# A two-layer graph kernel: row gathers, weight loads, fills and scatter lag of the first layer re-timed

## The reference, cut to what matters

```python
h = relu(layernorm(x))
x = x + layer0(h)      # x_norm = layernorm(h) * g + b
                       # q, k, v = x_norm @ Wq.T + bq, ...; dk, dv = silu(edge_attr @ Wd.T + bd)
                       # attn = silu(sum(q[dst] * k[src] * dk)) * cosine_cutoff(edge_weight)
                       # h + segment_sum(v[src] * dv * attn, dst) @ Wo.T + bo
h = relu(layernorm(x))
x = x + layer1(h)      # relu((A_norm @ (h @ W) + b) @ W1 + b1) @ W2 + b2, self-loops, symmetric norm
```

## Time and profile before

| what | us |
|---|---|
| median of 3 timed runs | 1825.09 (1824.55 to 1827.22) |
| the profiled execution's own time | 1813.87 |
| its span on the core | 1812.2 |
| PE busy | 1607.8 (89%) |
| DVE busy | 1424.0 (79%) |
| POOL busy | 1214.8 (67%) |
| ACT busy | 1127.9 (62%) |

### The profile page before, as it was taken

One profiled execution on the slowest core, in us unless ns is written; L12 is line 12 of the kernel. 1 busy time (PEld: TensorE's weight loads), 2 busy tenths in 40 slices (PEclk: granted clock), 3 DMA queues, 4 the chain that ended last, 5 costly groups with the idle time before them and its releaser, 6 DMA issues.

```text
span 1812.2 us, 29106 instructions
## 1 busy us (share of the span) xinstructions
PE 1607.8 (89%) x6406; PEld 1097.8 (61%) x6406; DVE 1424.0 (79%) x5625; ACT 1127.9 (62%) x2142; POOL 1214.8 (67%) x864
## 2 busy tenths in 40 slices
PE   6999999999999927677675099999999999999998
PEld 3556666666666615455553066677666666666776
DVE  8887877777777539888785788888888888888873
ACT  2345566666666402222222398889998889888884
POOL 5325888888887457888887766666666666666650
PEclk9999999999999968888887599999999999999999
DMA  9999666666666736656655889999999999999971
GB/s 373 417 416 342 158 188 195 191 183 184 184 192 194 206 73 117 116 127 112 128 110 107 201 222 268 265 272 271 266 272 265 273 264 271 267 264 270 274 223 77
DMA packets 148029, 398.73 MB, mean 220 GB/s; under 512 B 20144, under 2 KB 56756, under 8 KB 147974
## 3 DMA queue, kind: packets, MB, share of 16 engines
q1 hardware_dynamic: 88038, 278.61, 44.5%
q0 software_dynamic: 56416, 115.46, 33.8%
q10 hardware_dynamic: 3520, 4.07, 0.7%
HBM read 217.84 MB, written 180.23 MB: 220 GB/s over the span
## 4 chain that ended last, share of the span: by engine, by line
PE 53%; POOL 20%; DMA 11%; DVE 9%; issue 6%; SPq 1%; ACT 0%; POOLq 0%; DVEq 0%; ACTq 0%
PE bank L1394 11%; PE bank L1383 11%; POOL sums_dram L504 9%; PE bank L1278 8%; DMA out_dram<-cg 6%; PE bank L1271 4%; PE bank L1285 4%; PE bank L1320 4%; POOL kept L601 4%; POOL cg L508 4%; POOL b_rs L500 3%; PE bank L1373 3%; DMA sums_dram<-ub,sidx 2%; PE bank L1259 2%; DVE cg L995 2%
## 5 line engine op out<-in xcount | busy, mean ns | idle before, releaser
L1394 PE MATMUL bank<-w_sb,kept 128*128 128x256 f32 x1568 | 354.3, 379 | 0.0
L1383 PE MATMUL bank<-kept,w 128*128 128x512 f32 x784 | 353.3, 593 | 0.0
L601 POOL TENSOR_TENSOR kept<-kept 128x1024 f32<-128x1024 f32 x98 | 232.3, 2370 | 177.1 <-DVE cg L995 177.1
L1394 PEld LDWEIGHTS bank<-w_sb,kept 128*128 128x128 f32 x1568 | 298.1, 190 | 81.7 <-issue 46.3
L1347 PE MATMUL bank<-cg,en 128*128 128x256 f32 x386 | 130.4, 482 | 121.7 <-ACT cg L1148 67.1
L500 POOL TENSOR_TENSOR b_rs<-b_ve,minus_half 128x8 f32<-128x8 f32 x102 | 210.3, 2062 | 28.2 <-DVE b_ve L1012 28.2
L1383 PEld LDWEIGHTS bank<-kept,w 128*128 128x128 f32 x784 | 141.8, 191 | 140.9 <-issue 140.9
L1186 ACT ACTIVATE kept<-kept,b_nb,b_rs 128x256 f32<-128x256 f32 x392 | 202.2, 588 | 22.0 <-DVE b_nb L985 22.0
L1176 ACT ACTIVATE kept<-kept,b_nb,b_rs 128x256 f32<-128x256 f32 x392 | 202.3, 589 | 10.2 <-DVE b_nb L985 10.2
L504 POOL DMA_INDIRECT sums_dram<-ub,sidx x96 | 156.2, 1627 | 53.8 <-issue 27.0
L1347 PEld LDWEIGHTS bank<-cg,en 128*128 128x128 f32 x386 | 93.0, 248 | 153.8 <-issue 136.7
(11 more groups left out here) (179 smaller groups left out, 3355.8 us busy)
## 6 DMA issues: line engine op xcount, KB each, us to landing
sums_dram<-cg SPq DMA_DIRECT2D x196, 512.0 KB, 15.2
kept<-in_x_dram SPq DMA_DIRECT2D x97, 512.0 KB, 6.0
kept<-sums_dram POOLq DMA_DIRECT2D x97, 512.0 KB, 10.0
cg<-sums_dram SPq DMA_DIRECT2D x97, 512.0 KB, 8.5
out_dram<-cg SPq DMA_DIRECT2D x97, 512.0 KB, 10.0
row_k<-keys_dram SPq DMA_DIRECT2D x24, 256.0 KB, 4.5
row_s<-in_src_dram SPq DMA_DIRECT2D x24, 256.0 KB, 4.3
row_d<-in_dst_dram SPq DMA_DIRECT2D x41, 128.0 KB, 3.9
```

Source lines behind the costliest of these rows:

```text
L601: pool.tensor_tensor(X1[k.slot(8)], X[k.slot(4)], H[k.slot(2)], ALU.add).then_inc(g_xh, 1)
L1383: ins = pe.matmul(bank[:, 2 + m, :], w01[:, c, m * P:(m + 1) * P], hT[k.slot(2)][:, c * GN:(c + 1) * GN], start=(c == 0), stop=(c == KC - 1))
L1394: ins = pe.matmul(to, rT[k.slot(2)][:, c * GN + j * P:c * GN + (j + 1) * P], w2_sb[:, c, :], start=False, stop=(c == KC - 1), skip_group_c ...
```

## The change

Five things are edited. Between them they move no product, and leave the second and third stage alone.

- **Gathers ahead.** The destination rows (`kept`) of pairs 10 to 18 are gathered in POOL's steps 4 to 8, two pairs a step (one in step 8), behind the power; steps 10 to 18 gather the source rows alone. Source and destination rows get semaphores of their own, and DVE waits for the second only before it reads them.
- **Late weights.** `w2` (256 KB) and `b2_rows` (512 KB) are loaded by ACT's queue in step 14, not at the start.
- **Fills.** The `sums1` fills start with SP's step 10, three a step for 32 steps, and two more behind that.
- **Scatters.** The lag is 9 pairs up to POOL's step 24, which scatters two pairs, then 8; step 40 scatters two pairs again, then the lag is 7. The loop over p ends two steps earlier.
- **DVE's loop** is split in two, since what it waits for changes at pair 19.

```diff
 SCATTER_LAG = 9
+CATCH_UP = (24, 40)
+AHEAD_FROM, AHEAD_TO, AHEAD_STEP = 10, 19, 2
...
+            def fill_sums1(at, count):
+                for i in range(count):
+                    sp.dma_start(sums1[bass.ds(at + i * GN, GN), :].rearrange("(p j) d -> p (j d)", j=G),
+                                 rows_0).then_inc(s_fill1, 16)
...
-            run_steps(sp, EP, LATER, 2, LOADED - LATER, load_edges, start=LATER)
+            full = NG // 3 // 2 * 2
+            with sp.Fori(LOADED // 2, (LOADED + full) // 2) as reg:
+                for u in range(2):
+                    s = Step(u, reg, 2)
+                    load_pair(sp, s)
+                    fill_sums1(s.value(-LOADED, 3 * GN), 3)
+            fill_sums1(full * 3 * GN, NG - full * 3)
+            for k in range(LOADED + full, EP):
+                load_pair(sp, Step(k))
...
                     gather(XS[k % 4], x, node_i[:, k, 1:2], last_node, m_x[p % 2])
-                    gather(kept[:, k, :], x, node_i[:, k, 0:1], last_node, m_x[p % 2])
+                    if not AHEAD_FROM <= p < AHEAD_TO:
+                        gather(kept[:, k, :], x, node_i[:, k, 0:1], last_node, m_k[p % 2])
+
+            def gather_ahead(p):
+                first = AHEAD_FROM + AHEAD_STEP * (p - 4)
+                for k in range(2 * first, 2 * min(first + AHEAD_STEP, AHEAD_TO)):
+                    gather(kept[:, k, :], x, node_i[:, k, 0:1], last_node, m_ahead)
+
+            def scattered(p):
+                return min(EP, max(0, p - SCATTER_LAG + sum(p > c for c in CATCH_UP)))
...
-                k = p - SCATTER_LAG
-                if 0 <= k < EP:
+                if 4 <= p < AHEAD_FROM:
+                    gather_ahead(p)
+                for k in range(scattered(p), scattered(p + 1)):
...
-            for p in range(EP + SCATTER_LAG):
+            for p in range(EP + SCATTER_LAG - len(CATCH_UP)):
...
-                    dve.wait_ge(m_x[q], a.turns(2, 64))
+                    dve.wait_ge(m_x[q], a.turns(2, 32))
...
-            pe.wait_ge(s_ldw, 96)
+            pe.wait_ge(s_ldw, 80)
```

More of the change, by code:

```diff
@@ L261, in build @@
                                     "idx msg S ST U UB").split()]
-        m_sc = sem("m_sc")
+        m_sc, m_ahead, m_k = sem("m_sc"), sem("m_ahead"), sems("m_k", 2)
+        assert 2 * AHEAD_TO * D <= EC * D - early[0]
         C0 = [CG[1][:, 2 * i:2 * i + 2, :].rearrange("p a d -> p (a d)").rearrange("p (c d) -> p c d", d=D)
@@ L716, in pair_of, with messages @@
                 return t[(slice(None), bass.ds(k.value(0, 2), 2), *i)]
-            def messages(s):
+            def messages(s, late=False):
                 a, g, z, m, f = s.back(1), s.back(2), s.back(3), s.back(4), s.back(5)
@@ L722, in messages @@
                     q = a.slot(2)
-                    dve.wait_ge(m_x[q], a.turns(2, 64))
+                    dve.wait_ge(m_x[q], a.turns(2, 32))
                     for i in range(2):
                         dve.bn_stats(st1[q][:, 0, i, :], XS[2 * q + i])
+                    if late or a.reg is None and a.off >= AHEAD_TO:
+                        dve.wait_ge(m_k[q], a.turns(2, 32, 1 - len(range(AHEAD_FROM + q, AHEAD_TO, 2))))
+                    elif a.reg is None and a.off < AHEAD_FROM:
+                        dve.wait_ge(m_k[q], a.turns(2, 32))
+                    else:
+                        dve.wait_ge(m_ahead, 32 * (AHEAD_TO - AHEAD_FROM))
                     for i in range(2):
@@ L863, in messages @@
                     inverse_roots()
-            run_steps(dve, EP, MESSAGE_STEPS, 2, 6, messages)
+            assert AHEAD_FROM % 2 == 0 and AHEAD_TO % 2 == 1 and MESSAGE_STEPS + 6 < AHEAD_TO
+            static = (MESSAGE_STEPS + 7) // 2
+            for k in range(2 * static):
+                messages(Step(k))
+            with dve.Fori(static, (AHEAD_TO + 1) // 2) as reg:
+                for u in range(2):
+                    messages(Step(u, reg, 2))
+            with dve.Fori((AHEAD_TO + 1) // 2, (EP - 1) // 2) as reg:
+                for u in range(2):
+                    messages(Step(u, reg, 2), late=True)
+            for k in range((EP - 1) // 2 * 2, EP + MESSAGE_STEPS):
+                messages(Step(k))
             dve.wait_ge(m_keep, EP)
@@ L1037, in _ @@
             act.dma_start(wd_t[:, :], wd_in).then_inc(s_ldw, 16)
-            for t, w in ((w_t, w_in), (w1_raw, w1_in), (wo_t, wo_in), (w2_sb, w2_in)):
+            for t, w in ((w_t, w_in), (w1_raw, w1_in), (wo_t, wo_in)):
                 act.dma_start(t[:, :, :], w.rearrange("(c p) k -> p c k", p=P)).then_inc(s_ldw, 16)
-            act.dma_start(b2_rows[:, :], b2.rearrange("(a d) -> a d", a=1).broadcast_to([P, G * D])).then_inc(s_b2, 16)
             act.wait_ge(s_qkv, 32)
@@ L1051, in messages @@
                     act.activation(cut[:, :], cut[:, :], ACT.Sin, bias=half_pi[:, 0:1], scale=-1.0).then_inc(s_cos, 1)
+                if s.reg is None and s.off == LOADED + 4:
+                    act.dma_start(w2_sb[:, :, :], w2_in.rearrange("(c p) k -> p c k", p=P)).then_inc(s_b2, 16)
+                    act.dma_start(b2_rows[:, :], b2.rearrange("(a d) -> a d", a=1).broadcast_to([P, G * D])
+                                  ).then_inc(s_b2, 16)
                 if s.reg is None and s.off == len(HOT_STEPS) + 1:
@@ L1200, in nodes @@
                     if not k.past(2):
-                        act.wait_ge(s_b2, 16)
+                        act.wait_ge(s_b2, 32)
                         act.wait_ge(g_bits, 1)
```

1 line of the change is left out of this document (added).

## The result

The changed kernel takes 1837.65 us (median of 4 runs, 1835.63 to 1838.5), the kernel before 1825.92 on the same chip: a ratio of 1.0066, 95% interval 1.005 to 1.0082. It is slower by 11.7 us. I had forecast +2.5 us, 1827.6, with a range of 1816 to 1833; the result lies 4.7 us above it.

The account below looks back on a forecast made before the run. PE was taken to pace the first layer's loop at 10.83 us a step, with queued scatters as its tail. Tail -12.5, start -1.6 and catch-ups +16.6 gave +2.5 us, so 1827.6, range 1816 to 1833.

Parts of the forecast that it names:

- The tail: Scatters queued at the first layer's end: with no late fills and lag 7, the second layer's first gather comes 12.5 us earlier.
- Three fills a step: nothing by themselves: First layer's loop: a third fill raises the DMA share from 0.66 to some 0.78 and makes nobody wait; 0 us.
- The catch-ups: POOL's steps 24 and 40: second scatter pairs wait for landings and stop PE 5.4 and 7.8 us; with clock, 16.6 lost.
- two-fill landing of 7.58 us: Catch-up landing if the third fill doesn't hold back the scatter: delays 9.5 us each, whole change +1.3 us.
- the lateness carried over: Second catch-up: POOL, 4.7 us late after the first, wins back 2.3 and is still 2.4 late, so PE stands 7.8.
- the loss of clock: After PE's pause at each catch-up a lowered granted clock loses about 1.7 us of work, counted twice.
- rival of hidden catch-ups: Catch-ups in steps 24 and 40 mostly hidden: the change is worth -6.6 us, 1818.5, or 1811 if free; chance 0.32.
- my chance for "faster": Chance 0.32 that the whole kernel gets faster, given to the case of mostly hidden catch-ups.
- The start and the gathers ahead: Start: late weights let DVE's first statistics begin earlier, 1.6 us gained; gathers in steps 4 to 8: 0, with 1 either way.
- Three fills in the loop: First layer's loop: scatters land within the 8.88 us between pairs despite a third fill, so nobody waits; 0 us.
- rival of a scatter-bound loop: SP's 32 three-fill steps: landings beyond 8.88 us, at 9.2 costing some 10 us in all, 1837; chance 0.09.
- its gather "near 664": Second layer's start: POOL's first gather of sums_dram near 664 us, from 649.2 plus 16.6 less 1.6.

Follow-up runs that it names:

- changed_again: The changed kernel, unedited, run once more on another chip: 1823.22 us, ratio 1.0050 to the kernel before.
- fills_and_weights: The changed kernel without catch-ups and without gathers ahead; three fills a step, late weights and the second VectorE loop stay: 1811.13 us, ratio 0.9982 to the kernel before.
- fills_unsplit: The kernel before with only three fills a step and late weights, VectorE's program left as a single loop: 1804.70 us, ratio 0.9946.
- changed_padded: The changed kernel with 118 scratch writes in VectorE's program between the layers, shifting the code behind them: 1820.50 us, ratio 1.0033 to the kernel before.
- late_weights_only: The kernel before with only w2 and b2 loaded in step fourteen, not at the start: 1814.91 us, ratio 1.0000.
- no_catch_ups: The changed kernel with its two catch-ups taken out, one pair scattered a step throughout: 1813.17 us, ratio 0.9988 to the kernel before.
- ahead_old_fills: The changed kernel without catch-ups and with the old sums1 fills, two a step from step four: 1823.79 us, ratio 1.0046 to the kernel before.
- before_two_loops: The kernel before with VectorE's first-layer loop written as two loops of the same body: 1820.18 us, ratio 1.0029.

## Why the prediction was wrong

In the trace of changed_again (span 1819.4 for 1812.2) the change costs 7.2 us, and the terms of the sum can be laid beside it.

**The tail: right in size, -12.5 forecast, -11.3 measured.** From TensorE's last product with Wo to the second layer's first gather it was 27.97 us before (633.71 to 661.68) and is 16.68 now (648.46 to 665.14). First TensorE in the kernel before and in the changed one, then POOL's timeline, for the earlier trace rows:

```profile
633.71 1.97 PE L1320 MATMUL bank<-wo_t,stt 128*128 128x256 f32 x8 [0.78 <-ACT en L1079]
...
648.46 1.96 PE L1359 MATMUL bank<-wo_t,stt 128*128 128x256 f32 x8 [0.78 <-ACT en L1118]
...
659.15 1.55 POOL L509 DMA_INDIRECT sums_dram<-ub,sidx  x1 [3.08 <-DMA sums_dram<-en,sidx]
...
665.14 1.10 POOL L513 DMA_INDIRECT cg<-sums_dram,node_i  x1 [2.59 <-DMA sums_dram<-ub,sidx]
```

What I did not do was share it out. The same stretch is 20.9 us in fills_and_weights, so the fills alone, whose last are issued by 549 us in the changed kernel and not from 605 on the earlier trace rows, give 7.1 of it, and the catch-ups 4.2 to 5.0. "Three fills a step: nothing by themselves" was true of the loop, where SP's third fill left every step at 10.83 us, but not of the kernel: they are most of its gain, and SP's late burst of ten fills was what they took away. The tail of fills_unsplit, with nine pairs left, runs free:

```profile
613.77 1.54 POOL L509 DMA_INDIRECT sums_dram<-en,sidx  x1 [3.26 <-DMA sums_dram<-en,sidx]
...
620.24 1.55 POOL L509 DMA_INDIRECT sums_dram<-ub,sidx  x1 [3.08 <-DMA sums_dram<-en,sidx]
...
652.56 1.10 POOL L513 DMA_INDIRECT cg<-sums_dram,node_i  x1 [2.46 <-DMA sums_dram<-ub,sidx]
```

**The catch-ups: +16.6 forecast, 17.1 measured.** The landing at the first, from a pair's second scatter to the next pair's first, was 8.14 us (forecast 8.2):

```profile
321.55 1.83 POOL L509 DMA_INDIRECT sums_dram<-en,sidx  x1 [0.31 <-issue]
329.69 1.55 POOL L509 DMA_INDIRECT sums_dram<-ub,sidx  x1 [6.32 <-DMA sums_dram<-en,sidx]
331.54 1.55 POOL L509 DMA_INDIRECT sums_dram<-ub,sidx  x1 [0.30 <-issue]
332.57 1.92 POOL L563 TENSOR_TENSOR rs<-ve,minus_half 128x6 f32<-128x6 f32 x1
```

At the second catch-up it was 8.34. The two-fill landing of 7.58 us, at which the Trainium skill's rule of turns between queues (DMA: Bandwidth & Descriptors, Queues, rings and completion order) would have left it, was passed by 0.6 and 0.8. The same two landings are 9.23 and 8.01 in changed_padded, so one trace doesn't settle tenths; and no run here changed the fills alone at a catch-up, so what the third fill has in that isn't shown.

TensorE's pauses stand where they were forecast, near 335 and 518 us, each with a second one in the next step, when VectorE waits 2.97 us for gathers that were issued late:

```profile
335.49 1.13 PE L1324 MATMUL bank<-qkv_w,zT 128*128 128x256 f32 x4 [2.89 <-DVE at L764]
...
346.93 0.76 PE L1340 MATMUL bank<-eq,msg 128*128 128x128 f32 x2 [2.25 <-DVE msg L775]
...
518.37 2.08 PE L1324 MATMUL bank<-qkv_w,zT 128*128 128x256 f32 x4 [3.21 <-DVE at L764]
...
529.56 0.49 PE L1340 MATMUL bank<-eq,msg 128*128 128x128 f32 x2 [1.02 <-DVE msg L775]
```

Windows of 30 us over them show both parts of the loss, pauses and clock:

```profile
330.00:360.00 30.00, 24.72 (x90) 16.44 (x89) 17.64 (x90) 14.16 (x32) 25.40 (x20) 0.89 0.66 183
510.00:540.00 30.00, 25.77 (x100) 17.49 (x99) 17.03 (x85) 14.34 (x32) 23.53 (x18) 0.89 0.62 179
```

At the first, 5.3 us of idle time and 0.11 x 24.72 = 2.7 of lower clock; at the second 4.2 and 2.8. By TensorE's products with Wo the first cost 9.3 us (2.3 us ahead of the kernel before up to it, 7.0 behind it after) and the second 7.8 (14.8 behind, up to the last product). That is 1.3 and 0.8 us more than the windows show, and where these lie stays open. The forecast was 7.1 and 9.5. So the mechanism and the total were right; the first was 2.2 us dearer and the second 1.7 cheaper. What was wrong in it is the lateness carried over: I had POOL still 2.4 us late at the second, but TensorE's second pause, in the step after the first, had taken all of it, and the loss of clock was 2.7 and 2.8 us, not 1.7. The rival of hidden catch-ups is dead, and nearly all of my chance for "faster" with it.

**The start and the gathers ahead: -1.6 and 0 forecast, -2.3 measured in the trace up to step 23.** The start is 1.2 us early at POOL's first power, 29.90 for 31.10, but that gain alone is lost again (late_weights_only, 1.0000). Some 1.1 us more come in steps ten to thirteen; in changed_padded they don't, and TensorE is 0.8 us ahead there. By the times the gathers ahead win nothing: no_catch_ups is 0.06% slower than fills_and_weights. That is my 0, but my reason for it leaned rightly on the twelve early fills being gone: with them (ahead_old_fills) it is not 0.

**Three fills in the loop: 0, and 0 measured.** In no_catch_ups every step from 15 to 47 lasts 10.82 or 10.83 us. The rival of a scatter-bound loop, which would have given the measured 1837 on the first chip, did not happen: a good time for a wrong reason.

Up to the second layer's first gather all this comes to -11.3 + 17.1 - 2.3 = +3.5 us (665.14 for 661.68), where my sum has +2.5 and its gather "near 664".

**The step that failed is a cost that the sum put at nothing: the second loop in VectorE's program.** The prediction prices the gathers ahead at 0, counts nothing for the separate waits on the kept rows, and stops at the end of the first layer; the list of the change says that the second and third stage are left alone. But the waits need a second loop in VectorE's program, its code grows by 138 instructions, and 445 us after the first layer's end the jump into the last stage's loop waits 5.5 us: +4.3 us in the last stage (748.0 for 743.7). before_two_loops shows the cost by itself (+5.6 us, 1.0016 to 1.0042), changed_padded takes the wait away with the loop in place, and fills_unsplit is 6.5 us faster by the ratios than its like with two loops. Then 3.5 - 0.6 in the second layer + 4.3 = 7.2, the difference of the spans.

The ratios, one part added to the other, say the same: fills and weights 0.9946, with the second loop 0.9982 (6.5 us more), with the gathers ahead 0.9988 (1.1), with the catch-ups 1.0050 (11.2, where 16.6 less their 4.2 to 5.0 of the tail was to be expected). Only the loop's part is far from its forecast.

With it the forecast would have been +7, 1832, within the range; the measured ratios, 1.0050 and 1.0066, are +9 and +12 us. The interval of the first begins at +6.4 and holds the +7, that of the second begins at +9.1 and does not. The second comes from the chip of the unnamed waits, and what more the change costs there stays open. The loop's wait isn't the whole difference elsewhere either: changed_padded, without it, is still +6.0 us (4.2 to 8.0) over the kernel before, not +2.5. Its trace has the catch-ups at 16.6, as forecast, but only 10.0 in the tail and 0.8 before the catch-ups.

**Open.** Why the first profiled execution of the changed kernel held up VectorE's message 28 times and ScalarE's `ds` 21 times on something unnamed. It is the only trace of the changed kernel from that chip, and its time, 1837.41, is no outlier among the four there (1835.63 to 1838.5). The kernel before too was 11 us slower in the timed runs there (1825.92 for 1814.8) than elsewhere, while my trace of it took 1813.87. That the waits and the slower times belong together was not tried.

## What to carry to other kernels

Share a gain out among the edits that bring it before adding their costs: here one edit (no late burst of fills) earned 7 of the 11 us of the tail; the catch-ups, which earned the rest, cost 17, and the gathers ahead earned nothing and brought the second loop. An edit that grows a program can be paid for in a loop that it does not touch; after such an edit look for a single wait on `issue` at each later loop's first instruction. And compare a surprising row with a second profile of the same kernel before building on it: an 8 us theory rested on one execution.

## What the hardware showed that I had not expected

A pair's landing, from its second scatter to the next pair's first, is 4.6 us when nothing else moves (615.62 to 620.24 in fills_unsplit) and mostly 8.0 to 8.4 in the loop with three fills a step, whether POOL is silent behind the pair (8.14, 8.34) or issues gathers (8.44); the longest at a catch-up was 9.23 (changed_padded, 323.06 to 332.29). A step leaves 8.88 us for it, so about 0.5 us is all by which a scatter can usually move forward in one step without a wait.

One jump into a loop cost VectorE 4.9 to 6.2 us in the traces of all six kernels whose code ahead of the loop was 232 or 233 instructions over a multiple of 256 (the changed kernel in both of its traces), and nothing in the other seven kernels, at 94 or 95; it happened once in an execution, at the loop's entry. Only these two places were tried.
